# A gated Flamingo block on one core: the work that prepares a batch, spread over a whole attention period and started one batch earlier

## What is computed

```python
x = x + tanh(g_xattn[0]) * attend(LN(x), ctx, ctx)      # A: one head of 256, additive mask
x = x + tanh(g_ffn[0])   * self_attend(LN(x))           # B: 4 of 16 heads of 64, chosen by a router on the mean token
x = x + tanh(g_xattn[1]) * attend16(LN(x), ctx, ctx)    # C: 16 heads of 16, 512 queries x 1601 keys
x = x + tanh(g_ffn[1])   * experts(LN(x))               # D: 8 experts, each token goes to one; 256 -> 1024 -> 256
```

## Time and profile before

| | |
|---|---|
| median of 3 runs | 3713.0 us (3712.45 to 3713.04) |
| the profiled execution, its own time | 3709.8 us |
| its span, first to last instruction | 3708.0 us |
| TensorE busy, granted clock | 2991.8 us (81%), mean 0.897 of 2.4 GHz |
| VectorE, ScalarE, GpSimd busy | 1686.3, 1460.7, 286.2 us |
| lead-in, up to the first `scores_t` | 325.4 us |
| periods of batches 0 to 7 | 376.3, 384.7, 385.6, 385.9, 385.8, 386.2, 364.8, 207.6 us |
| from the last `scores_t` to the end | about 505 us |

### The profile page before, as it was taken

One profiled execution on the slowest core, in us unless ns is written; L12 is line 12 of the kernel. 1 busy time (PEld: TensorE's weight loads), 2 busy tenths in 40 slices (PEclk: granted clock), 3 DMA queues, 4 the chain that ended last, 5 costly groups with the idle time before them and its releaser, 6 DMA issues. The chain is left out here.

```text
span 3708.0 us, 38607 instructions
## 1 busy us (share of the span) xinstructions
PE 2991.8 (81%) x13228; PEld 1350.7 (36%) x13228; DVE 1686.3 (45%) x4029; ACT 1460.7 (39%) x2794; POOL 286.2 (8%) x330
## 2 busy tenths in 40 slices
PE   5648887888878987898788878887888788649992
PEld 3323332333233332333243323332333232248882
DVE  2226364636554564546544654464536666201111
ACT  2112354434543454435443544353435455412220
POOL 1110010001010100010000010001000000030003
PEclk7867898989997999899889988998999999879996
DMA  5221112111121213121221132013111211145655
GB/s 208 48 74 29 36 42 80 50 41 42 52 72 41 46 29 79 54 46 32 70 65 30 30 88 65 21 33 88 48 35 36 53 36 25 52 164 184 202 186 164
DMA packets 188798, 257.54 MB, mean 69 GB/s; under 512 B 43189, under 2 KB 163357, under 8 KB 187846
## 3 DMA queue, kind: packets, MB, share of 16 engines
q1 hardware_dynamic: 174028, 190.24, 19.1%
q0 software_dynamic: 14592, 65.05, 5.2%
HBM read 193.23 MB, written 61.62 MB: 69 GB/s over the span
## 5 line engine op out<-in xcount | busy, mean ns | idle before, releaser
L1570 DVE TENSOR_REDUCE mxC<-PS 128x1 f32<-128x400 f32 (+1 forms) x2048 | 1093.3, 570 | 1057.5 <-PE PS L1124 1047.6
L802 ACT ACTIVATE reg<-PS 128x512 f32<-128x512 f32 (+1 forms) x1664 | 971.0, 598 | 1398.8 <-PE PS L1156 1395.6
L1124 PE MATMUL PS<-reg 96*128 96x400 bf16 (+1 forms) x2048 | 724.8, 363 | 224.1 <-DVE mxC L1570 163.1
L1156 PE MATMUL PS<-reg 99*128 99x512 bf16 (+1 forms) x1664 | 659.3, 405 | 39.4 <-ACT reg L802 32.9
L1124 PEld LDWEIGHTS PS<-reg 96*128 96x128 bf16 x2048 | 207.8, 101 | 801.6 <-DVE mxC L1570 614.7
L1171 PE MATMUL PS<-reg 128*17 128x512 f32 (+1 forms) x3328 | 489.7, 664 | 0.0
L1156 PEld LDWEIGHTS PS<-reg 99*128 99x128 bf16 (+1 forms) x1664 | 168.8, 104 | 333.0 <-ACT reg L802 149.0
L877 PE MATMUL PS<-reg 128*128 128x512 f32 (+1 forms) x512 | 205.5, 527 | 1.7 <-DVE small L1347 1.0
L829 ACT ACTIVATE reg<-PS,reg 128x256 f32<-128x256 f32 x192 | 80.6, 471 | 318.2 <-PE PS L1256 318.2
L901 PE MATMUL PS<-reg 128*128 128x512 f32 (+1 forms) x416 | 196.4, 607 | 2.1 <-ACT reg L682 2.1
L888 PE MATMUL PS<-ident,reg 128*128 128x128 f32 (+1 forms) x416 | 101.4, 374 | 98.7 <-ACT reg L679 97.6
(11 more groups left out here) (181 smaller groups left out, 2587.0 us busy)
## 6 DMA issues: line engine op xcount, KB each, us to landing
reg<-in_D_W SPq DMA_DIRECT2D x48, 1024.0 KB, 6.4
reg<-in_A_mask POOLq DMA_DIRECT2D x32, 800.5 KB, 5.8
dramK<-reg SPq DMA_DIRECT2D x144, 100.0 KB
reg<-in_ctxT POOLq DMA_DIRECT2D x8, 1601.0 KB, 7.1
reg<-in_ctx POOLq DMA_DIRECT2D x8, 1536.0 KB, 7.7
dramQ<-reg SPq DMA_DIRECT2D x96, 128.0 KB
reg<-dramQ SPq DMA_DIRECT2D x32, 384.0 KB, 6.1
reg<-dramK SPq DMA_DIRECT2D x32, 300.4 KB, 4.3
```

The costliest lines, as they stand in the source:

```text
L802: act.activation(pr[u % RING][0:r, :], PS[0:r, s_bank(g, v), :], ACT.Exp).then_inc(a_expC, 1)
L1124: last = mm(PS[:, bank, 0:w], qs[(NG * bb + g) % 3][0:ROWS, h, t * P:(t + 1) * P], ks[g % 2][0:ROWS, h, c0:c0 + w], start=True, stop=True)
L1156: last = mm(PS[0:r, bank, :], ks[g % 2][0:STK, h, c * P:c * P + r], qs[(NG * b + g) % 3][0:STK, h, :], start=True, stop=not with_mask)
L1570: v.tensor_reduce(mxC[:, h, t, j:j + 1], PS[:, MB[i % 2], 0:M_CH[j][1]], AX.X, ALU.max).then_inc(v_mx, 1)
```

## The change

The pieces and their arithmetic stay. What moves:

- The tables are new. A chain now reaches over two periods: in period b, `start_next` does norm A, query piece, the A scores and the first 12 `turn_a` of batch b+2 in steps 143 to 205; `prepare` does the rest of batch b+1 in steps 2 to 141; `give_out` finishes batch b-1 in steps 2 to 42. Score and transposing pieces of A alternate; the pieces of `weigh_a` stand two steps apart, `score_b` four instead of three.
- `project_v` is done for batch b+1 in period b, steps 34 to 47, after `out_a`. ACT copies each piece into a small double buffer vs, SP stores it to a DRAM tensor dramV (`store_v`), and SP loads it back into vc in two parts, at step 184 of period b and at step 3 of the next (`load_v`). `evac_v` waits until the piece before last has been stored.
- The key pieces stand at 52 to 64 and 124 to 133, before the query projection. The queries are split and stored by halves (`store_q(n, m)`). POOL loads ctx at step 158 and waits there for the stores alone; the `split_k` are over by then.
- aoT now lies in the memory of xT, and FIRST of the fourth group is 5 instead of 11.
- The lead-in is now two emptier periods (b = -2 and the first three groups of b = -1), then the fourth group of b = -1 with the chunks of batch 0 and A of batch 1 between them.

```diff
-
-U_V = list(range(VP))
-U_O1, U_O2 = (8, 10), (12, 14)
-U_S = [16 + i for i in range(8)] + [31 + i for i in range(8)]
-U_T = [23, 24, 25, 26, 27, 28, 29, 30, 38, 39, 40, 41, 43, 45, 46, 48]
-U_PV = [50 + i for i in range(10)]
-U_XD, U_GATE, U_OA = (53, 56), 58, (62, 63)
-U_XB, U_RL = (73, 75), 78
-U_K = [67, 76, 80, 84, 160, 163, 166, 169]
-U_QB, U_KB, U_VB = (94, 95), (97, 98), (100, 101)
-U_SB = [103 + 3 * k + 3 * (k >= 4) for k in range(8)]
-U_TB = [U_SB[i // 2] + (4, 6)[i % 2] for i in range(16)]
-U_PVB, U_OB, U_XC, U_QC = (120, 135), (137, 138), (148, 150), (152, 153)
-U_XA, U_QG = (180, 183), (187, 190)
+FIRST, LAST = (3, 3, 3, 5), (43, 43, 43, 44)
+
+U_PV = [10 + 2 * i for i in range(10)]
+U_O1, U_O2, U_OA = (11, 13), (15, 17), (30, 32)
+U_XD, U_GATE = (31, 33), 36
+U_V = [34, 36, 38, 40, 42, 45, 47]
+U_XB, U_RL = (44, 46), 50
+U_K = [52, 56, 60, 64, 124, 127, 130, 133]
+U_QB, U_KB, U_VB = (70, 71), (73, 74), (76, 77)
+U_SB = [80 + 4 * k + 2 * (k >= 4) for k in range(8)]
+U_TB = [U_SB[i // 2] + (5, 7)[i % 2] for i in range(16)]
+U_PVB, U_OB, U_XC, U_QC = (101, 119), (121, 122), (132, 134), (136, 138)
+U_XA, U_QG = (151, 153), (155, 157)
+U_S = [164, 166, 168, 170, 174, 176, 178, 180, 187, 189, 191, 193, 199, 201, 203, 205]
+U_T = [175, 177, 179, 181, 185, 188, 190, 192, 198, 200, 202, 204, 2, 4, 6, 8]
+N_LO = 6
...
-        R = 47536
+        R = 47536 - 1024 + 1088
...
         oc = take([S], F32)
         ao = take([QT, D], F32)
-        aoT = take([KD, S], F32)
+        aoT = xT
...
+            def store_q(n, m):
+                sp.wait_ge(v_qs, 2 * n + m + 1)
+                for r, part in enumerate(QPART):
+                    sp.dma_start(dramQ[n, 8 * m:8 * m + 8, r * DC:(r + 1) * DC, :],
+                                 qp[:, part, m, :]).then_inc(qd_stored[m], 16)
+
+            def store_v(n, i):
+                sp.wait_ge(a_vp, VP * n + i + 1)
+                c = min(2, CT - 2 * i)
+                sp.dma_start(dramV[n, :, 2 * i:2 * i + c, :], vs[:, i % 2, 0:c, :, :]).then_inc(v_stored[i % 2], 16)
+
+            def load_v(n, c0, c1, signal):
+                sp.wait_ge(v_stored[0], 64 * (n + 1))
+                sp.wait_ge(v_stored[1], 48 * (n + 1))
+                sp.dma_start(vc[:, c0:c1, :, :], dramV[n, :, c0:c1, :]).then_inc(signal, 16)
...
+                if u == 3 and b >= 0:
+                    past(sp, pe_pv, UN * b)
+                    load_v(b, N_LO, CT, vc_hi)
...
+                if u == 184 and n < B:
+                    past(sp, pe_pv, UN * b + 3 * CT + N_LO)
+                    load_v(n, 0, N_LO, vc_lo)
...
+                            store_v(n, i)
                     if u == U_RL + 4:
                         gather_heads(n)
-                    if u == U_QC[1] + 4:
-                        store_q(n)
-                    if u == U_QC[1] + 5:
+                    if u == U_QC[0] + 5:
+                        store_q(n, 0)
+                    if u == U_QC[0] + 8:
                         load_q(n, 0)
-                    if u == U_QC[1] + 8:
-                        load_q(n, 1)
+                    if u == 153:
+                        store_q(n, 1)
                     for i in range(2 * NCH):
...
+            def start_next(m, u):
+
+                if m and u == U_OA[1] + 3:
+                    pool.wait_ge(v_oA, QT * m)
+                    load_x(m)
+                if m and u == U_PVB[1] + 1:
+                    pool.wait_ge(pe_pvB, 2 * m)
+                    load_mask(m, 0)
+                    load_mask(m, 1)
+                if m and u == U_K[-1] + 2:
+                    pool.wait_ge(pe_kp, 8 * m)
+                    pool.wait_ge(pe_vp, VP * m)
+                    load_ctxT(m)
+                if u == U_XA[0] - 5:
+                    root(norm_a(m))
+                if m and u == 158:
+                    for i in range(KD):
+                        pool.wait_ge(qd_stored[i], 16 * NR * m)
+                    load_ctx(m)
+                if u == U_T[3] + 1:
+                    pool.wait_ge(pe_ptA, 16 * m + 4)
...
+            def evac_v(n, i):
+                act.wait_ge(pe_vp, VP * n + i + 1)
+                past(act, v_stored[i % 2], 16 * ((4, 3)[i % 2] * n + i // 2))
+                bank = (F0, F1)[i % 2]
...
-                past(pe, v_kr, 8 * n)
+                past(pe, v_tq, 2 * n - 1 + m)
...
-                    pe.wait_ge(v_oA, QT * n + 2 * u + 2)
+                    pe.wait_ge(a_vp, VP * (n + 1))
                 elif u in (NCH, NCH + 1):
-                    pe.wait_ge(v_tq, 2 * n + u - NCH + 1)
+                    pe.wait_ge(v_oB, QT * n + 2 * (u - NCH) + 2)
                 else:
...
+                pe.wait_ge(v_kr, 8 * n + 7 + m)
                 for k in range(KD):
...
+            def turn_o(e, k):
 
                 if k == 0:
                     pe.wait_ge(g_ab, e + 1)
-                    pe.wait_ge(a_xT, 2 * LD)
+                    if e < B - 2:
+                        pe.wait_ge(a_ptA, 16 * (e + 3))
+                    elif e == B - 2:
+                        pe.wait_ge(a_xT, 2 * norm_b(B - 1) + 4)
+                    else:
...
-            def project_v(b, i):
-
-                if i == 0:
-                    pe.wait_ge(v_kr, 8 * b + 8)
-                    if b < B - 1:
-                        pe.wait_ge(a_qg, 2 * b + 4)
-                elif i >= 2:
-                    pe.wait_ge(a_vp, VP * b + i - 1)
+            def project_v(n, i):
+
+                if i < 2:
+                    pe.wait_ge(v_oA, QT * n + 2 * i + 2)
+                else:
+                    pe.wait_ge(a_vp, VP * n + i - 1)
                 for c in range(2 * i, min(2 * i + 2, CT)):
                     for k in range(KD):
                         last = mm(PS[0:rows(c), FB[i % 2], c % 2 * D:(c % 2 + 1) * D],
...
                     past(pe, v_ao, NG * bb + g)
-                if g == 0 and c % 2 == 0:
-                    pe.wait_ge(a_vp, VP * bb + c // 2 + 1)
+                if g == 0 and c == 0:
+                    pe.wait_ge(vc_lo, 16 * (bb + 1))
+                if g == 0 and c == N_LO:
+                    pe.wait_ge(vc_hi, 16 * (bb + 1))
...
-            def iteration(b, with_mask):
-                n, ab, o = b + 1, b < B - 1, b > 0
-                LD, LB, LC, LA = norms(b)
-                for u in range(NU):
-                    g, v = u // UN, u % UN
-                    ahead = chunks(g, v) if g < NG - 1 or ab else ()
-                    nb, ng = (b, g + 1) if g < NG - 1 else (n, 0)
-                    if v == MT[g] and (g < NG - 1 or ab):
...
             def attend(with_mask):
-                for i in range(NSC):
-                    scores_c(0, 0, i, with_mask)
-                transpose_m(0, 0, SB[1])
+                for u in range((NG - 1) * UN, NU):
+                    step(-1, u, with_mask)
                 for b in range(B):
-                    iteration(b, with_mask)
```

More of the change, by code:

```diff
@@ new lines, in _ @@
+            for b in range(-2, B + 1):
+                for u in range(NU):
+                    if b >= 1:
+                        give_out(b, u)
+                    if 0 <= b < B and u == 27:
+                        keep_residual(b)
+                    if 0 <= b + 1 < B:
+                        prepare(b + 1, u)
+                    if b + 2 < B:
+                        start_next(b + 2, u)
+                    if b == -1 and u == 68:
+                        pool.wait_ge(v_mT, 2)
+                        pool.partition_all_reduce(small[:, 32:33], small[:, 20:21], P,
+                                                  bass.bass_isa.ReduceOp.max).then_inc(g_set, 1)
@@ L1113, in scores_c, with start_next @@
+            def start_next(m, u):
+                for k in range(KD):
+                    if u == U_XA[k]:
+                        turn_x(norm_a(m), k)
+                    if u == U_QG[k]:
+                        project_qg(m, norm_a(m), k)
+                for i in range(16):
+                    if u == U_S[i]:
+                        score_a(m, i)
+                for i in range(12):
+                    if u == U_T[i]:
+                        turn_a(m, i)
             def scores_c(bb, g, i, with_mask):
@@ new lines, in step @@
+            def step(b, u, with_mask):
+                g, v = u // UN, u % UN
+                nb, ng, ahead = ahead_of(b, u)
+                if v == MT[g] and 0 <= nb < B:
+                    past(pe, a_expC, NU * b + u - 1)
+                    transpose_m(nb, ng, SB[((UN + 1) * g + MT[g]) % 2])
+                if 0 <= b < B:
+                    scores_t(b, g, v, nb < B, with_mask)
+                for i in ahead[:1]:
+                    scores_c(nb, ng, i, with_mask)
+                if 0 <= b < B:
@@ L1222, in _ @@
             for u in range(NU):
-                fill(u, 0, True, False, 3, 1, 2, 0)
+                start_next(0, u)
+            for u in range((NG - 1) * UN):
+                step(-1, u, False)
             pe.wait_ge(v_mf, 1)
```

813 lines of the change are left out of this document (377 added, 436 removed).

## The result

The changed kernel takes 3392.7 us (3385.6 to 3400.7, 4 runs) against 3712.7 us before: ratio 0.9147, 95% interval 0.9117 to 0.9178, or 320 us less. Predicted were 3403 us, 310 less. The profiled execution has a span of 3383.8 us, 324 less than before.

What follows compares the result with a forecast made beforehand. No engine is full; TensorE, nearest, idles about 62 us a period, waiting on where chain pieces stand. Savings of 226 (batches 0 to 5), 61, 10 and 13 (lead-in) make 310 us: 3713 to 3403 us, range 3300 to 3555.

Steps and rivals of the forecast that it cites:

- the blocked queue: POOL waits 34.70 us before the ctx load; key splits, stores and ACT's exponentials stand behind it.
- Bare steps and the chain's excess: Steps without chain pieces, priced from batch 7: 1.03 us with chunks, 0.72 without; the chain costs some 180 us a period.
- Part 1: A's scores and transposes: alternating them removes waits for bank F2, saving 14.6 us a period (0 to 24).
- Part 2: Second half of the key pieces: moved before the ctx load, saving 15 us in batches 0 to 5, 6 in batch 6.
- Part 3: B: scores four steps apart instead of three let eight bare steps hide waits, saving 6 us (0 to 8.3).
- Part 4: Chunks of the fourth group: FIRST at 5 instead of 11 lowers their density, saving 4 us (0 to 5).
- Part 5: V through memory: stores and loads are covered by slack, costing nothing; project_v keeps its price, one period ahead.
- Rival 3: Slower: the store of V holds up ACT through evac_v's waits, giving 3750 us; chance 0.04.
- Part 6: New near waits, for the third query tile's mask and A's last exponential: together 2 us lost (0 to 10).
- Batches 6 and 7: Batch 6 falls 61 us, as A's first half leaves it; batch 7 falls 10 us, losing project_v.
- rival 5: Slower: small pauses of a spread chain bring TensorE's clock to 0.75, about 4010 us; chance 0.01.
- The lead-in: Before the first scores: nothing stands behind the ctx load any more, ending at 312, saving 13 us (-10 to 30).

Runs made afterwards that it cites:

- e1: Kernel before the change, with POOL issuing the next ctx load at step 196 instead of 161, out of the key splits' way; ratio 0.9841, 59 us less.
- e2: Changed kernel with A's score pieces and fourth-group transposes in rows again instead of alternating; ratio 0.9475, 3509.8 us.
- e6: Changed kernel with the ten weigh_a pieces in ten consecutive steps (19 to 28) instead of two steps apart; ratio 0.9201.
- c1: The changed kernel itself, unedited, run a second time as a measure for others on the same chip; ratio 0.9166.
- e4: Changed kernel with B's transposes 4 and 6 steps after their scores instead of 5 and 7; ratio 0.8926, 3310.1 us.
- e11: The kernel of e4, unedited, run a second time as a measure; ratio 0.8911, 3302.2 us.
- e5: Changed kernel with FIRST of the fourth group at 11 again instead of 5; ratio 0.9174.
- e7: Changed kernel without V's way through memory: stores, loads and their waits left out, value tile holding ones; ratio 0.9135.
- e9: Kernel of e4 with the second half of the query projection at 141 instead of 138 and the next batch's norm and query piece four steps later; ratio 0.8945.
- e3: Changed kernel with B's score pieces three steps apart instead of four, transposes 4 and 6 steps after them, weighing at 97 and 112; ratio 0.9179, 3403.3 us.
- e8: Kernel of e4 with the first four key pieces at 49, 54, 59, 64 instead of 52, 56, 60, 64; ratio 0.8930.

## Why the prediction was right

The time (3403 against 3392.7) and the cause, a chain that waited because of where its pieces stood, were right. That the time came so near is in part luck. Batches 0 to 5 gave 265 us instead of 226; batches 6 and 7, the lead-in and the tail gave 59 instead of 84. Within a full period B and the steps with new chunks came out some 13 us worse than priced, and the rest some 20 us better. Of the 320 us, the blocked queue (59 us, e1) and the places of A's pieces (117 us, e2) are shown by runs; the rest, a little under half, was not taken apart by runs beyond the 15 to 20 us of e6. Point by point:

- **Bare steps and the chain's excess.** The base of the sum held: steps 164 to 207 of batch 6 are 36 steps with chunks and 8 without, by my prices 36 x 1.03 + 8 x 0.72 = 42.8 us, and take 43.64.
- **Part 1** was right in kind and too small. The term that was mis-sized is the exposure of the long exponentials and the price of a score piece: 31.1 us priced, 21.7 measured; no run says how much of it is the one and how much the other. The saving is 23.3 us a period against my 14.6, and e2 shows 16 of them. The clock in A's stretch is 1.00, as predicted.
- **The rule on transposes** (the Trainium skill, "TensorE: Matmul & The Clock Gate", Part 4: PE-mode transpose: they don't count as busy for the clock gate). e2's stretch has the same matmuls and transposes as the changed kernel's, and only their places differ: 0.88 against 1.00. By that rule, the trace agrees as far as rows of transposes with waits between them fall to the lower clock; it does not separate the transposes from the waits.
- **Part 2** was right in its cause: e1 takes the stretch from 34.4 to 23.8 us and a period down by 9.6 us, which is its lower bound, for the blocked queue alone. In the changed kernel the wait of `high_k` is gone from the second half (0.6 us in batch 3), and that half with the query projection and the norms is 23.6 us a period cheaper, where parts 2 and 4 had 19. The 14 us beyond the blocked queue were not taken apart. 3.4 us of wait stay in the first half, whose four pieces now stand four steps apart instead of four to nine; I had looked only at the second.
- **Part 3** is the step that failed, though spacing itself helps. I took the waits between B's scores, exponentials and transposes as slack to be filled, and didn't lay the lists of ACT side by side: 5 and 7 steps after scores that are four apart, seven of sixteen copies fall into the step of the next exponentials, and the new kernel also puts the exponentials first there, which the kernel before did not. That cost 9 to 11 us a period (73.6 and 74.4 us in the changed kernel and c1, 64.2 and 63.2 in e4 and e11); with it removed, B is within 3 us of where I had it (61.9). My own sign of being wrong, B's 40 steps at 62 plus 6 us or more, did show.
- **Part 4** was too large: 0.8 us a full period and 2.3 in batch 6 by e5's stretches, where I had 4. The row I took it from has no pieces of A in it, and I left out what the steps cost that get chunks anew.
- **Part 5** held: 2.1 us for a store, two short waits in the lead-in and none in a period, and nothing that shows in e7. Rival 3 is out (and its 3750 was added up wrong: 40 waits at 9 us more than the 7 that are covered make 360, so 3763).
- **Part 6** cost nothing in the periods, where I had 2 us. Both near waits, of the transposes for the long exponential (line 699; 7.0 us before matmuls) and of DVE for a mask (5.0 us), stand in the lead-in alone.
- **Batches 6 and 7.** Batch 6 came out 11 us long by B's collision. Batch 7 should have lost 10 us with V and lost nothing. Its first 52 steps took 65.92 us at a clock of 1.00 with V in them, and take 68.35 us at 0.88 without it but with the norm and gate, which stood in steps 53 to 58 before and stand in 31 to 36 now:

```profile
2994.68:3060.60 65.92, 58.94 (x308) 24.66 (x304) 39.42 (x91) 34.99 (x63) 5.38 (x3) 1.00 0.18 41
```

```profile
2669.25:2737.60 68.35, 57.86 (x280) 18.40 (x277) 41.11 (x108) 32.37 (x59) 5.37 (x3) 0.88 0.21 54
```

28 matmuls fewer, and nearly the same busy time. Cut finer, V did leave: steps 0 to 9 are 8.0 us shorter. Steps 20 to 29 are 3.5 us longer with the same 43 matmuls, at a clock of 0.87 and with 2.9 us of waits for the maxima, beside DVE's work for the norm; steps 30 to 39, where norm and gate stand now, 5.1 us longer; steps 40 to 51 are 2.1 us longer with the same 50 matmuls, at 0.75. In e9 the same 52 steps ran at 0.95 and took 65.3 us, so the low clock is some 3 of the missing 10 us, and the rest is where norm and gate stand. Why the clock falls here was not tried. Of rival 5 this much came true: whole spread periods ran at 0.96 to 0.98, but single stretches lie lower, steps 140 to 155 at 0.84 and B at 0.94 in the mean.
- **The lead-in**: 315.0 against 312, though e1 shows that the 28 us wait was not to be had alone (5.7 us); the rest came with the new order.

## What to carry to other kernels

When pieces are set between the steps of a paced loop, write down for every engine what stands in the same step: a follow-up that falls behind other work of the same engine can stall the first engine of the loop, and moving it by one step was worth as much as a quarter of the whole rewrite. When a rewrite changes how the lists are emitted, check the order within a step too. Don't let pieces of one kind that share a buffer stand in a row; alternate them with pieces that don't need it. Check the total and the parts separately: here A came out 9 us a period better and B 12 us worse, and the total showed neither. And don't read one batch for all: the first readings of B, of e3 and of e8 rested on batch 3, which was the shortest period of one kernel and the longest of another.

## What the runs showed of the hardware

The same work takes longer at the lower clock, but a wait of one length was not always followed by it. B's first weighing, 16 matmuls, took 5.20 us at a granted clock of 0.70 in batch 3, behind a wait of 2.28 us; in batch 6 it stood behind the same wait and ran at 1.00:

```profile
2523.87 3.65 PE L1016 MATMUL PS<-reg 128*64 128x512 f32 x16 [2.28 <-ACT reg L732]
```

The clock of one stretch is no measure of the time of the whole. With the waits of B removed (e11), a period lost 7.6 us of idle time and 2.2 us of busy time. e8 brought steps 52 to 69 from 0.90 to 0.95 in the mean, and the period came out less than 1 us shorter. In e2, where rows of waits run through the stretch, batch 3 lost about as much to the clock as to the waits: 70.9 against 62.6 us of busy time for the same 302 matmuls, beside 12.3 against 2.8 us idle.
